# Token attention of an eight-layer kernel: the two halves of the softmax half a period apart, statistics drawn further ahead

## The reference

```python
q = _split_qk(x @ Wq.T, b, n) * SCALE      # 32 half heads of 8 numbers for each token
k = _split_qk(x @ Wk.T, b, n)
v = (x @ Wv.T).reshape(b, n, H, 2 * D).transpose(0, 2, 1, 3)
att = jnp.einsum('bnqd,bnkd->bnqk', q, k)   # 32 x 32 for each token
att = jax.nn.softmax(jnp.nan_to_num(att).astype(jnp.float32), axis=-1)
diff = att[:, :, :H, :H] - lam * att[:, :, H:, H:]
out = jnp.einsum('bnah,bhnd->bnad', diff, v)
out = out * jax.lax.rsqrt(jnp.mean(out * out, axis=-1, keepdims=True) + EPS)
out = (out * (1.0 - LAM_INIT)).reshape(b, n, DIM)
return out @ Wo.T + bo
```

## Time and profile before

| | us |
|---|---|
| median of 3 runs (1413.53 to 1423.64) | 1413.91 |
| the profiled execution | 1416.3 |
| its span, first to last instruction | 1414.4 |
| TensorE busy | 1056.7 |
| VectorE busy | 708.2 |
| ScalarE busy | 391.9 |
| GpSimd busy | 314.1 |
| mean granted TensorE clock | 0.819 |

### The profile page before, as it was taken

One profiled execution on the slowest core, in us unless ns is written; L12 is line 12 of the kernel. 1 busy time (PEld: TensorE's weight loads), 2 busy tenths in 40 slices (PEclk: granted clock), 3 DMA queues, 4 the chain that ended last, 5 costly groups with the idle time before them and its releaser, 6 DMA issues.

```text
span 1414.4 us, 21459 instructions
## 1 busy us (share of the span) xinstructions
PE 1056.7 (75%) x8114; PEld 925.5 (65%) x8114; DVE 708.2 (50%) x1426; ACT 391.9 (28%) x711; POOL 314.1 (22%) x352
## 2 busy tenths in 40 slices
PE   3689885577888755788858999567777767459998
PEld 2467653466777644565548999556777766349998
DVE  3578744535454354876636444344454444324443
ACT  2156652222332311333232322111112221112222
POOL 5200001345436532111113000100222222420000
PEclk9689987789999986977658999856666665569999
DMA  8644300000010001744100000155656565100000
GB/s 243 190 145 147 122 3 1 0 8 23 31 46 0 1 0 53 224 134 128 60 1 1 1 1 1 48 103 99 108 100 103 111 112 83 30 0 16 16 16 16
DMA packets 147430, 89.39 MB, mean 63 GB/s; under 512 B 109632, under 2 KB 136256, under 8 KB 146560
## 3 DMA queue, kind: packets, MB, share of 16 engines
q1 hardware_dynamic: 142576, 69.40, 20.3%
q10 hardware_dynamic: 3328, 13.63, 5.0%
q0 software_dynamic: 1424, 4.98, 1.1%
HBM read 54.16 MB, written 33.55 MB: 62 GB/s over the span
## 4 chain that ended last, share of the span: by engine, by line
PE 52%; DVE 21%; issue 7%; ACT 6%; POOL 6%; SPq 5%; DMA 3%; ACTq 0%; POOLq 0%; DVEq 0%
PE SC L375 16%; PE pb L375 8%; PE SC L1742 6%; PE pa L375 6%; PE OT L1617 3%; SPq L548 3%; DVE mx L1144 3%; POOL hr L713 2%; PE SC L1601 2%; PE SC L1574 2%; DVE ON L1479 1%; DVE Qs L1483 1%; DVE xT_l L1413 1%; POOL rstd L680 1%; ACT Qs L1046 1%
## 5 line engine op out<-in xcount | busy, mean ns | idle before, releaser
L678 POOL TENSOR_SCALAR ve<-mv 128x2 f32<-128x2 f32 x64 | 14.1, 221 | 709.1 <-DVE mv L1400 484.7
L375 PE MATMUL SC<-xT_h,w_h 128*128 128x256 f32 x512 | 145.1, 283 | 2.8 <-DVE xT_l L1413 2.8
L375 PE MATMUL SC<-xT_l,w_h 128*128 128x256 f32 x512 | 144.6, 282 | 0.0
L375 PE MATMUL SC<-xT_h,w_l 128*128 128x256 f32 x512 | 144.4, 282 | 0.0
L1742 PEld LDWEIGHTS SC<-Ks,b_Q 96*128 96x128 f32 x512 | 111.6, 310 | 2.2 <-issue 2.2
L1742 PE MATMUL SC<-Ks,b_Q 96*128 96x32 f32 x512 | 112.4, 374 | 0.6 <-DMA Ks<-k_groups 0.6
L375 PEld LDWEIGHTS SC<-xT_h,w_h 128*128 128x128 f32 x512 | 99.2, 194 | 3.6 <-DVE xT_l L1413 3.6
L1144 DVE TENSOR_REDUCE mx<-SC 128x4 f32<-128x1024 f32 x64 | 78.1, 1220 | 40.9 <-PE SC L1574 40.8
L375 PEld LDWEIGHTS SC<-xT_l,w_h 128*128 128x128 f32 x512 | 98.3, 192 | 0.0
L375 PEld LDWEIGHTS SC<-xT_h,w_l 128*128 128x128 f32 x512 | 98.2, 192 | 0.0
L1479 DVE TENSOR_TENSOR ON<-SC,ON 128x512 f32<-128x512 f32 x64 | 43.7, 683 | 106.0 <-ACT ON L1038 105.9
(11 more groups left out here) (365 smaller groups left out, 2876.5 us busy)
## 6 DMA issues: line engine op xcount, KB each, us to landing
Qs<-q_stack SPq DMA_DIRECT2D x56, 128.0 KB, 3.0
k_stack<-KT_h SPq DMA_DIRECT2D x16, 256.0 KB, 2.3
k_stack<-KT_l SPq DMA_DIRECT2D x16, 256.0 KB, 2.8
q_stack<-QT_h SPq DMA_DIRECT2D x16, 256.0 KB, 2.2
q_stack<-QT_l SPq DMA_DIRECT2D x16, 256.0 KB, 2.8
Ks<-k_groups ACTq DMA_DIRECT2D x8, 512.0 KB, 13.7
o_groups<-b_O ACTq DMA_DIRECT2D x8, 512.0 KB, 3.2
Qs<-q_stack SPq DMA_DIRECT2D x56, 64.0 KB, 3.0
```

The source lines that it names most:

```text
L375: ins = pe.matmul(out_ap, left[a], right[b], start=first and n == 0, stop=last and n == len(terms) - 1)
```

## The change

Only offsets in the token stage, and the order of TensorE's lines within a round, are changed. No operation, tile, wait or DMA is added or removed. The half h of scores, less_maximum, exp and weights stands 4 h rounds behind half 0 instead of 1 h. The statistics of a batch stand 18 rounds ahead of its scores instead of 15, its deviation 17 instead of 15, and the bias row moves from 14 to 12 ahead. The attends stand in rounds 10 and 11 instead of 7 and 8. The loads of Q and K move from 7 to 4 rounds ahead and that of V from round 1 to 5, both still behind the same scores. What comes after the attends moves by two or three rounds.

```diff
@@ sync @@
-                        for b in due(g, -7):
+                        for b in due(g, -4):
                             load_q(b)
-                        for b in due(g, 1):
+                        for b in due(g, 5):
                             load_v(b)
-                        for b in due(g, 14):
+                        for b in due(g, 16):
                             load_out(b)
@@ gpsimd @@
-                        for b in due(g, 16):
+                        for b in due(g, 18):
                             clipped(b)
-                        for b in due(g, 17):
+                        for b in due(g, 19):
                             token_heads(b)
-                        for b in due(g, -15):
+                        for b in due(g, -12):
+                            row_bias(b)
+                        for b in due(g, -17):
                             rstd_of(b)
-                        for b in due(g, -14):
-                            row_bias(b)
@@ scalar @@
-                    for b in due(g, -7):
+                    for b in due(g, -4):
                         load_q(b)
                         load_k(b)
                     for h in range(TT):
-                        for b in due(g, 7 + h):
+                        for b in due(g, 10 + h):
                             heads_out(b, h)
-                        for b in due(g, 1 + h):
+                        for b in due(g, 1 + 4 * h):
                             probs(b, h)
@@ vector @@
-                        for b in due(g, 1 + h):
+                        for b in due(g, 1 + 4 * h):
                             less_maximum(b, h)
-                        for b in due(g, 3 + h):
+                        for b in due(g, 3 + 4 * h):
                             weights_of(b, h)
-                    for b in due(g, 17):
+                    for b in due(g, 19):
                         square_sums(b)
-                    for b in due(g, -15):
+                    for b in due(g, -18):
                         stats(b)
@@ tensor @@
                     for b in due(g, 8):
-                        attend(b, 1)
-                    for b in due(g, 0):
-                        scores(b, 0)
-                    for b in due(g, 1):
-                        scores(b, 1)
-                    for b in due(g, 20):
+                        turned(b, 1)
+                    for h in range(TT):
+                        for b in due(g, 4 * h):
+                            scores(b, h)
+                        for b in due(g, 10 + h):
+                            attend(b, h)
+                    for b in due(g, 24):
+                        y_out(b)
+                    for b in due(g, 5):
+                        turned(b, 0)
+                    for b in due(g, 22):
                         a_turned(b)
                     for b in due(g, -13):
                         x_turned(b)
                     for b in due(g, -12):
                         q_out(b)
-                    for b in due(g, 5):
-                        turned(b, 0)
                     for b in due(g, -11):
                         k_out(b)
-                    for b in due(g, 6):
-                        turned(b, 1)
                     for b in due(g, -10):
                         v_out(b)
-                    for b in due(g, 22):
-                        y_out(b)
-                    for b in due(g, 7):
-                        attend(b, 0)
```

More of the change, by code:

```diff
@@ L954, in tokens @@
                     for h in range(TT):
-                        for b in due(g, 7 + h):
+                        for b in due(g, 10 + h):
                             heads_out(b, h)
-                        for b in due(g, 1 + h):
+                        for b in due(g, 1 + 4 * h):
                             probs(b, h)
-                    for b in due(g, 6):
+                    for b in due(g, 8):
                         turned(b)
-                    for b in due(g, 8):
+                    for b in due(g, 11):
                         store_out(b)
-                    for b in due(g, 16):
+                    for b in due(g, 18):
                         squares(b)
-                    for b in due(g, 20):
+                    for b in due(g, 22):
                         high(b, aT, OT[1], "aT", "y", 1, "ah")
@@ L1332, in tokens @@
                         low(b, KT, pa, "kh", "kl")
-                    for b in due(g, 23):
+                    for b in due(g, 25):
                         residual(b)
-                    for b in due(g, -15):
+                    for b in due(g, -18):
                         stats(b)
```

## The result

The changed kernel takes **1432.7 us** (median of 4 runs, 1428.2 to 1437.2) against 1413.8 for the kernel before in the same series: a ratio of **1.010, 95% interval 1.006 to 1.015** (it is formed over all runs, those of before from 1413.5 to 1423.6, and so is a little under the quotient of the medians). The forecast was 1430, with a range of 1415 to 1440. So it is slower, by half a per cent to one per cent.

What follows compares the result with a forecast made beforehand. The prediction took a chain of waits, headed by GpSimd's long step, to bound the kernel, with no engine full. Periods +9.9, start +1.8 and drain +4.8 gave +16.5 on the median 1413.9: 1430 us, range 1415 to 1440.

Steps and rivals of the forecast that it cites:

- seven periods: Token stage, first scores of batch 0 to those of batch 7: 271.9 us against 262.0, +9.9.
- start of the stage: Token stage before the first scores: ScalarE's first load issue comes behind x_high of batch 1, +1.8 us.
- drain: Token stage from the last scores 0 to the last residual add: 68.5 us against 63.7, +4.8.
- the stage: Whole token stage: periods, start and drain together +16.5 us.
- The full one: A full period of the token stage's new loop: 40.4 us, 20.15 of it between scores 1 and scores 0.
- The last period: Seventh period, no batch fetched: 33.95 us, with loads at 14.9, the shorter kind; 18.6 was the other end.
- the present bound is GpSimd's long step: Kernel before, token stage: GpSimd's power of an older batch (5.46 us) stands in front of a small step, the deviation.
- The issues hold nothing: Rival, ScalarE's DMA issues: Q high gets in at 3.0 us, loads decide, period 37.7 to 38.9; 1414 to 1425 us; 10%.
- time 0: Token stage's loop: the end of a batch's second scores, from which the prediction counts its steps.
- TensorE at 2.4 GHz: Rival, turned 1 and transposes at full clock: 1.2 to 1.3 us a period less, 1418 to 1424 us; 20%.
- The loads later: Rival, K's loads land after 20.15; at 22 us a period is 42.3, total 1438 to 1447 us; 10%.
- A real gain: Rival, token stage: removed waits count in full, 35.1 us a period, 16 us less, 1399 us; 4%.

Runs made afterwards that it cites:

- e2: The changed kernel with statistics, deviation and bias row back at their old offsets (15, 15 and 14 rounds ahead); 1448.1 us, ratio 1.017 to the kernel before.
- e3: The changed kernel with VectorE making Q low behind the second half's softmax instead of ahead of it; 1428.5 us, ratio 1.003 to the kernel before.
- e7: The changed kernel with all of Q's loads issued by SP and only K's two DMAs by ScalarE; 1410.5 us, ratio 0.990 to the kernel before.
- e9: The kernel before, unaltered, run and profiled again; 1421.5 us, ratio 1.000, stage 359.9 us.
- e5: The changed kernel, unaltered, run again in a second series; 1429.4 us, ratio 1.005 to the kernel before.
- e6: The changed kernel with ScalarE making Q high ahead of its share of the loads instead of behind it; 1439.1 us, ratio 1.009 to the kernel before.
- e1: The kernel before with only the statistics' changed offsets, softmax halves still side by side; 1417.9 us, ratio 0.998 to the kernel before.
- e8: e4 with SP issuing V's loads behind the stores and load_out; 1376.0 us, ratio 0.965 to the kernel before.
- e4: The kernel before reordered: halves side by side, both attends behind both scores, statistics 24 rounds ahead, x normalised 19 ahead; 1379.0 us, ratio 0.969.
- e11: e8 with all of Q's loads on SP and the head sums two rounds later, behind half 0's weights; 1364.1 us, ratio 0.957 to the kernel before.
- e10: e1 with all of Q's loads on SP; 1397.2 us, ratio 0.984 to the kernel before.

## Why the prediction was right

**The mechanism** was read rightly and is shown: e2 puts the cost on the distance of the halves, and e3 and e7 take two of its parts away. In e3 turned 1 comes 4.5 us sooner and the loads take over most of that; in e7 the gain is clear in the time as well (0.990 against 1.005 in the same series).

**Term by term**, forecast and then measured:

| term | forecast | measured |
|---|---|---|
| seven periods | +9.9 (271.9 against 262.0) | +8.2 (270.1 against 261.9) |
| start of the stage | +1.8 | +3.9 |
| drain | +4.8 | +5.9 (69.63 against 63.77) |
| the stage | +16.5 | +18.0; +12.5 against e9 |

The seven forecast periods add up to 271.8, not 271.9, which changes nothing.

*The periods.* The full one was forecast at 40.4 and is 39.2 to 39.6. In the one of the timeline above, scores 1 start 12.6 after scores 0 (13.15 forecast), and scores 0 of the next batch 19.6 after scores 1 end (20.15): the weights begin 0.35 sooner, because VectorE's operations overlap a little, and scores 0 start 0.25 before turned 1 is over. The last period went the other way: 35.7 against 33.95. K's last part landed 16.2 us after scores 1 where I took 14.9, the short end of two that I had kept for the range:

```profile
1195.33 7.09 PE L1742 MATMUL SC<-Ks,b_Q 96*128 96x32 f32 x32 [2.81 <-issue]
```

In e5 the same period is 38.6 (18.3), so the choice of the short end was wrong both times, and +8.2 is the sum of two errors that partly cancel. In the six full periods TensorE did not wait for K at scores 0, as costed. But K's last part had landed only 0.1 to 2.0 us before; e3 shows the wait as soon as turned 1 comes earlier.

*The start.* This term was mis-sized. I had ScalarE's first issue 1.8 later; it came 16.9 after the stage's start instead of 14.1, which is 2.8, and K's last part then took 10.3 to land instead of 9.0. The changed kernel's rows:

```profile
903.95 0.60 ACT L902 ACTIVATE KT_h<-pa 128x512 fp32r<-128x512 f32 x1 [1.96 <-PE pa L375]
...
908.35 1.11 PE L1836 MATMUL pa<-ident,xn 128*128 128x128 f32 x4 [2.68 <-DVE xn L1271]
...
909.51 4.73 ACTq L930 DMA_DIRECT2D b_Q<-q_groups  x6
```

and one of before:

```profile
909.81 0.60 ACT L902 ACTIVATE KT_h<-pa 128x512 fp32r<-128x512 f32 x1 [0.85 <-PE pa L375]
```

K high of the first batch waits 1.1 us longer for its matmuls (11.35 after the start instead of 10.23), and everything behind it on VectorE, the next statistics among it, is late by as much. The transposes then took 1.11 us at a granted clock of 0.50 where the earlier trace rows has 0.66 at 1.00. TensorE ran slower here than in before; I had taken before's durations over. The other way, ScalarE's issues began together with the high part of x (909.50), not 0.60 behind it as I had counted.

*The drain.* Each step is within 0.3 us of the forecast up to the head sums, and 0.8 to 1.3 us late from there on: one operation of GpSimd's took 1.20 us here instead of 0.25, while VectorE worked through L1291 beside it:

```profile
1218.21 1.23 DVE L1291 TENSOR_TENSOR pr<-pr,m 128x1024 f32<-128x1024 f32 x1
1218.34 1.20 POOL L717 TENSOR_TENSOR hr<-hr,ssqe 128x32 f32<-128x32 f32 x1 [0.18 <-POOL ssqe L715]
```

Other runs show the same and separate it. This short operation (L717) takes 0.25 or 0.26 us wherever VectorE is not in L1291 or in the product L1304. In all 19 places where it falls beside one of them, in six of the profiles, it takes 0.59 to 1.26 and ends 0.11 or 0.12 us behind the VectorE instruction that it met; beside the low part of Q, whose one input is in PSUM, it stays at 0.25 (e6, e7). So it was held until that instruction was over. The long power (L713) takes 5.46 with and without such company. One of three in e3:

```profile
1066.69 1.26 POOL L717 TENSOR_TENSOR hr<-hr,ssqe 128x32 f32<-128x32 f32 x1 [0.18 <-POOL ssqe L715]
```

The Trainium skill (GPSIMD Engine Reference, Specifications) states that the SBUF interface of GpSimd is shared with VectorE and contends with instructions that have two SBUF inputs; L1291 has two, and the traces agree.

**What I read wrongly in the kernel before.** That "the present bound is GpSimd's long step" describes the chain, but taking the step away alone gains half a per cent at most (e1): ScalarE's issues stood right behind it. The rows said so already, since the exp started at the end of the issues. I used that row for the new order and not for the old one. The forecast did not suffer, since the gain of the removed waits was never added as a term of its own, but built into the new loop. The reason given for V's 10.81 us of issue, that its loads are cut very small, does not explain them either: the same eight loads are issued in 4.7 us for the last batch of the kernel before, and in 4.2 in e8.

**The rivals.** *The issues hold nothing* is refuted: ScalarE is free 5.8 us after time 0, and e7 gives back 3.1 us per period. The Trainium skill (Trainium Kernel Development and Optimization, Key Constraints) counts issuing from several engines only as a saving of issue time. By that e7 should have been no faster; it is 23.5 us faster in the stage, so the measurement decides. *TensorE at 2.4 GHz*: turned 1 took 1.97 at a granted clock of 0.50 behind 9.0 us without work, as forecast. The Trainium skill (TensorE: Matmul & The Clock Gate, Part 1) advises doing matmuls in one run ahead of a wait on DMA, so that the full clock is kept. The trace agrees, here with a wait on VectorE. The attends too are dearer, 24.1 us for all 512 matmuls against 15.6. In the kernel before they stand behind the projections and each half took 1.06 to 1.08 us at 1.00. Now they follow scores 0, and ten of the sixteen took 1.76 to 1.94 at 0.50 to 0.59; in e4 and e11, where they follow both scores, all 512 matmuls take 28.4 and 28.5. *The loads later* did not come: of the seven periods TensorE waited for K in the last alone, and there the loads landed at 16.2 (18.3 in e5), not 22. In the third they landed at 19.9, 0.1 before TensorE would have waited. *A real gain* was not in this order; e11 shows it in another.

**What stays open.** The ratio was 1.010 in one series and 1.005 in the other, and the stages ahead of the token stage, with the same code everywhere, end between 889.7 and 904.6 us. What makes these 15 us was not tested; it is as large as the change itself, so the whole run shows the change less clearly than the stage does. The medians are 18.9 us apart in the first series and 6.1 in the second, where 16 was forecast. That the first came so near is partly luck; the stage, 12.5 to 19.1 us longer by the four profiles, is the better witness.

## What to carry to other kernels

Before you remove the wait at the head of a chain, find what else ends at the same place: here GpSimd's step, ScalarE's DMA issues and V's loads each bounded the same period within a microsecond or two, and the first alone was worth next to nothing. An engine that computes something on the path should not issue DMAs that become possible just as its operand does; one queue with nothing else to do was better here than two. Moving one half of a softmax away from the other puts its latency on the loop once more and leaves TensorE idle ahead of it, while work of other batches placed around both halves gains without that.

## What the runs showed of the hardware that I had not expected

- K's last part landed in 6.5 us (median; 6.2 to 7.2) in e7, where Q's loads came from SP alone, against 12.6 (10.3 to 14.9) in the changed kernel, where both queues issued them at once; its issue on ScalarE took 0.51 instead of 0.70. The lines of the changed kernel and of e7:

```profile
L942 ACTq DMA_DIRECT2D Ks<-k_groups x8: 585/704/713, 914.8 to 1184.0; - x8
...
DMA to landing us min/median/max: 10.3/12.6/14.9
```

```profile
L943 ACTq DMA_DIRECT2D Ks<-k_groups x8: 512/512/624, 911.8 to 1161.2; - x8
...
DMA to landing us min/median/max: 6.2/6.5/7.2
```

- The twelve Q issues on SP took 8.3 to 8.8 us, against 4.1 to 4.7 for six on each of two queues. The loads as a whole were sooner all the same: where TensorE waited for Q itself in e11, it was there 12.5 and 15.5 us after scores 1, while K was there after 16.2 to 19.9 in the changed kernel. How much of this is the second queue, and how much that K's loads now stand ahead of Q's instead of behind them, no run separates; V's loads are a small part (11.4 in e8, where they are elsewhere).
- SP issued the eight V loads in 4.0 to 6.8 us in e7, and in 4.2 to 5.1 in e8, where they stand away from the split loads; right behind these it took 10.8 to 15.1 us in the kernel before and 12.0 to 16.0 in the changed one (4.7 and 5.0 for the last batch, whose V loads come later). From issue to landing they took 2.9 us (median) in e7 and e10 against 8.4 to 10.0 in before, the changed kernel and e4.
- Two executions of the same code differ by 5.6 us in this one stage (354.3 and 359.9), mostly in the last period, in V's landing and the attends behind it.
